# Post-norm transformer block on one core: both query halves of a step's fp32 probabilities-times-values product issued in one burst

## The reference, cut to what matters

```
result = (embeddings @ w_qkv).reshape(b, s, 3, 16, 32)
q, k, v = ...                                     # each [b, 16, s, 32]
scores = einsum('bnqd,bnkd->bnqk', q, k) / sqrt(512)
probs = softmax(scores, axis=-1)
ctx = einsum('bnqk,bnkd->bnqd', probs, v)
x = layernorm(x + ctx)
```

## Time and profile before

| what | value |
|---|---|
| median of three runs | 4508.9 us (4506.7 to 4509.33) |
| profiled execution: its span, first to last instruction | 4507.4 us (the profile gives no other time for it) |
| PE matmul busy | 4203.1 us, 93% of the span |
| DVE busy | 3206.1 us, 71% |
| ACT busy | 1857.5 us, 41% |
| L1320 (weigh), 4096 records | 531.1 + 523.5 us busy |
| L576 (maxima), 2080 records | 399.6 + 379.1 us busy |
| L492 (reductions of maxima), 2080 | 1386.7 us busy, 690 ns each |

### The profile page before, as it was taken

One profiled execution on the slowest core, in us unless ns is written; L12 is line 12 of the kernel. 1 busy time (PEld: TensorE's weight loads), 2 busy tenths in 40 slices (PEclk: granted clock), 3 DMA queues, 4 the chain that ended last, 5 costly groups with the idle time before them and its releaser, 6 DMA issues. The chain is left out here.

```text
span 4507.4 us, 59394 instructions
## 1 busy us (share of the span) xinstructions
PE 4203.1 (93%) x23081; PEld 1721.7 (38%) x23081; DVE 3206.1 (71%) x5179; ACT 1857.5 (41%) x2168; POOL 610.8 (14%) x670
## 2 busy tenths in 40 slices
PE   3499999999999999999999999999999999999999
PEld 2233344333533344333443334433353334433344
DVE  9856687667866678666876668766786667856688
ACT  3245433453334533445334543345333453344533
POOL 4300022001210012100220002200121001210022
PEclk8599999999999999999999999999999999999999
DMA  4110001010010100011001000101001010001100
GB/s 157 32 34 27 17 22 37 15 29 22 21 30 17 41 13 19 28 28 29 17 24 32 27 17 22 37 15 29 22 22 30 17 41 13 19 27 29 29 17 22
DMA packets 80509, 126.76 MB, mean 28 GB/s; under 512 B 21056, under 2 KB 23104, under 8 KB 80192
## 3 DMA queue, kind: packets, MB, share of 16 engines
q1 hardware_dynamic: 80192, 122.51, 9.4%
HBM read 53.22 MB, written 16.78 MB: 16 GB/s over the span
## 5 line engine op out<-in xcount | busy, mean ns | idle before, releaser
L492 DVE TENSOR_REDUCE mx<-R 128x1 f32<-128x512 f32 x2080 | 1386.7, 690 | 911.3 <-PE R L576 909.0
L1020 ACT ACTIVATE arena<-SC 128x1024 f32<-128x1024 f32 x1024 | 996.7, 1022 | 968.2 <-PE SC L1302 967.9
L1397 PE MATMUL SC<-wgu,split 128*128 128x512 f16 (+1 forms) x4608 | 935.5, 361 | 6.8 <-ACT split L1059 3.6
L1397 PEld LDWEIGHTS SC<-wgu,split 128*128 128x128 f16 x4608 | 445.9, 98 | 469.5 <-DVE arena L1192 10.2
L1320 PE MATMUL CT<-arena,v_even 128*33 128x512 f32 x2048 | 531.1, 606 | 9.1 <-ACT arena L1013 9.1
L1320 PE MATMUL CT<-arena 128*33 128x512 f32 x2048 | 523.5, 603 | 0.0
L1412 PE MATMUL CT<-wd,arena 128*128 128x512 bf16 x2112 | 476.7, 379 | 0.0
L946 POOL TENSOR_TENSOR x<-x,ctx_new 128x256 f32<-128x256 f32 x128 | 105.3, 823 | 2401.8 <-DVE ctx_new L1124 2401.8
L556 PE MATMUL R<-xT,wqkv 128*128 128x512 bf16 x1632 | 411.2, 385 | 1.5 <-ACT xT L454 1.3
L576 PE MATMUL R<-ks_even,qs_even 96*128 96x512 bf16 x1056 | 399.6, 400 | 8.0 <-DVE mx L492 2.9
L576 PE MATMUL R<-arena 96*128 96x512 bf16 x1024 | 379.1, 384 | 5.5
(11 more groups left out here) (111 smaller groups left out, 3749.9 us busy)
## 6 DMA issues: line engine op xcount, KB each, us to landing
x<-n_L_attn_embeddings_dram SPq DMA_DIRECT2D x136, 256.0 KB, 2.9
arena<-split SPq DMA_DIRECT2D x384, 64.0 KB, 2.0
out_dram<-x SPq DMA_DIRECT2D x64, 256.0 KB, 2.0
qs_even<-split SPq DMA_DIRECT2D x204, 64.0 KB, 2.0
ks_even<-split SPq DMA_DIRECT2D x204, 64.0 KB, 2.0
x<-in_L_ffn_w_up_dram SPq DMA_DIRECT2D x13, 256.0 KB, 2.8
x<-in_L_attn_w_qkv_dram SPq DMA_DIRECT2D x4, 768.0 KB, 6.6
x<-in_L_ffn_w_gate_dram SPq DMA_DIRECT2D x11, 256.0 KB, 4.5
```

The source lines that it names most:

```text
L492: nc.vector.reduce_max(mx[:, j:j + 1], ring_of(ring, n)[:, :], AX_X).then_inc(max_done, 1)
L1020: nc.scalar.activation(probs[:, s % 2, hd, :], SC[hd][:, :], ACT.Exp, scale=SCALE).then_inc(exp_done, 1)
L1397: last = nc.tensor.matmul(GU[kk % 2][which][:, 0:w], xhT[:, part_x * KH + k, :], wgu[:, part_w * KH + k, which * I + first:which * I + fir ...
```

## The change

`weigh` loses its argument `half` and issues both halves, four products, one after the other behind a single set of waits. It stands where the first half stood; in step 0 of a pair (from pair 1 on) that is ahead of the scores. Nothing is added or left out, and no other engine's list changes.

```diff
-                    def weigh(s, half):
+                    def weigh(s):
...
-                        if half == 0:
-                            pe.wait_ge(exp_done, 2 * s + 2)
...
+                        pe.wait_ge(exp_done, 2 * s + 2)
...
-                        key_tile, queries = step_half(p, t, half)
-                        for hd in range(2):
-                            last = nc.tensor.matmul(CT[2 * HD * hd:2 * HD * hd + HD + 1, queries * BANK:(queries + 1) * BANK],
...
-                        if half == HALVES - 1:
-                            last.then_inc(pv_done, 1)
+                        for half in range(HALVES):
+                            key_tile, queries = step_half(p, t, half)
+                            for hd in range(2):
+                                last = nc.tensor.matmul(
...
+                        last.then_inc(pv_done, 1)
...
                         if t == 0 and p >= 1:
-                            weigh(s - 1, 0)
+                            weigh(s - 1)
                             scores(p, t, 0)
                             run(places[0])
                             scores(p, t, 1)
                             run(places[1])
-                            weigh(s - 1, 1)
                             run(places[2])
                         else:
...
                             if s >= 1:
-                                weigh(s - 1, 0)
+                                weigh(s - 1)
                             run(places[2])
-                            if s >= 1:
-                                weigh(s - 1, 1)
                         run(places[3])
-                    weigh(len(steps) - 1, 0)
-                    weigh(len(steps) - 1, 1)
+                    weigh(len(steps) - 1)
```

More of the change, by code:

```diff
@@ L1306, in scores @@
                         last.then_inc(scores_done, 1)
-                    def weigh(s, half):
+                    def weigh(s):
                         p, t = divmod(s, TILES)
                         g = p // 2
-                        if half == 0:
-                            pe.wait_ge(exp_done, 2 * s + 2)
[L1314 to L1317, removed]
-                        key_tile, queries = step_half(p, t, half)
-                        for hd in range(2):
-                            last = nc.tensor.matmul(CT[2 * HD * hd:2 * HD * hd + HD + 1, queries * BANK:(queries + 1) * BANK],
-                                                    v[g % 2][:, key_tile, 2 * (p % 2) + hd, :],
-                                                    probs[:, s % 2, hd, half * BANK:(half + 1) * BANK],
-                                                    start=(key_tile == 0), stop=(key_tile == TILES - 1))
-                        if half == HALVES - 1:
-                            last.then_inc(pv_done, 1)
+                        pe.wait_ge(exp_done, 2 * s + 2)
+                        if t == 0 and g >= 1:
+                            pe.wait_ge(v_done, 2 * (ring.group(g) + 1))
+                        if t == 0 and p >= 1:
+                            pe.wait_ge(ctxT_done, p)
+                        for half in range(HALVES):
+                            key_tile, queries = step_half(p, t, half)
+                            for hd in range(2):
+                                last = nc.tensor.matmul(
+                                    CT[2 * HD * hd:2 * HD * hd + HD + 1, queries * BANK:(queries + 1) * BANK],
+                                    v[g % 2][:, key_tile, 2 * (p % 2) + hd, :],
+                                    probs[:, s % 2, hd, half * BANK:(half + 1) * BANK],
+                                    start=(key_tile == 0), stop=(key_tile == TILES - 1))
+                        last.then_inc(pv_done, 1)
                     def x_turn(i):
```

## The result

The changed kernel takes 4644.56 us (median of four runs, 4641.68 to 4646.69) against 4508.9 before: 1.0301 times as long, 95% interval 1.0286 to 1.0315. That is 136 us slower, 17 us in each of the 8 turns. The forecast was 4647 us.

A forecast was written before the change was run, and what follows sets the result against it. PE, 93% busy, was taken as the bound, with its order deciding where it waits for banks. The terms summed to 17.6 us a turn, 141 in 8 turns, less 2 hidden: 139 more, 4647 us; range 4600 to 4685.

The forecast's parts named there:

- bank time of 1.18: From a maximum's product to the next product that may use its bank: 1.18 us, DVE's 0.69 reduction included.
- pair 5: Steps 1 to 5 of this pair: +0.54 us each, 2.7 a turn; m4 starts 1.96 after m2.
- ordinary steps: 14 steps a turn: 4.65 us against 4.13, +0.52 each, 7.3 a turn.
- saved edge of 0.22: One edge of a burst fewer in a step when the two halves are joined: 0.22 us saved.
- Projection steps: 16 steps a turn: 0.30 us of waiting at the next m0 less 0.22 saved, +0.08 each, 1.3 a turn.
- Ends of pairs: Seven a turn: +0.43 us for three with a projection, +0.62 for three without, +1.32 behind pair 0; together 4.5.
- chain to neg: At a pair's end, from the start of the first of two last reductions to neg: 2.08 us, before 2.78.
- copy of CT and the exps: Behind pair ends without a projection, ACT is late for the next burst: +0.38 us, an estimate.
- wait for DMAs that the longer burst hides: Scores at a pair's start, held back by the maxima's DMAs: 2 us hidden in the whole run.
- Last pair: Its steps: +1.0 us; PE's wait for the first layer norm behind them: +0.85; sum 1.85 a turn.
- The third maximum: Rival: it doesn't wait for a bank, so 0.22 is saved in 512 steps, 112 us, 4396; chance 0.03.
- The clock: Rival: PE's clock drops to 1.2 GHz in ordinary steps and pair 5, 550 us slower, some 5060; chance 0.03.

The follow-up runs named there:

- newly dealt kernel: The kernel before with halves joined only in the 16 projection steps a turn, their maxima and projection parts dealt anew: 4486.55 us, ratio 0.9949.

## Why the prediction was right

- **The bank time of 1.18.** It was read from a place in pair 5 where two maxima and the next m0 stood together, and it is the wait between m2 and m4 in the ordinary steps and between m2 and m3 in pair 5. Shortening nothing but the reductions, from 0.69 to 0.23 us, brought it down to 0.71 and the loss of an ordinary step from 0.51 to 0.05, so for the banks that DVE empties the cause is shown, not only argued. For m4 in pair 5, whose bank ACT empties, the wait came as forecast (1.96 forecast, 1.95 measured), but no run changed ACT's copy.
- **The saved edge of 0.22** is there: 1.84 for two halves, and the newly dealt kernel keeps most of it.
- **Ordinary steps**: +0.52 forecast, +0.51 measured (4.64 for 4.13). **Projection steps**: +0.08 and +0.08 (6.80 for 6.73). **Pair 5**: +0.54 and +0.53. These are the steps in the middle of a run of their kind; at the seams a wait falls on the next step.
- **Ends of pairs**: the chain to neg 2.08 forecast, 2.07 measured. Steps 6 to 1 over pair 0 to pair 1 grew by 0.09 + 1.93 - 0.78 + 0.92 = 2.16, of which 0.51 is the ordinary step and 0.30 the projection's wait carried into step 6: 1.35 for a forecast of 1.32. The copy of CT and the exps hold up step 1 as estimated, 0.41 where 0.38 was written. All seven ends together, with the wait for DMAs that the longer burst hides, cost 4.0 a turn, where the sum has 4.5 less some 0.25.
- **Last pair**: steps 1 to 5 gained 0.94 (forecast 1.0), and from the last step to the next turn 0.75 on average (forecast 0.85).
- **The rivals.** The third maximum does wait. The clock stayed at 1.00 in a window with a wait of 0.57 us in every ordinary step and 1.03 at the neg job. The Trainium skill (TensorE: Matmul & The Clock Gate, "A second HAM failure mode: psum-queue depth-cycling") tells of a kernel whose clock swung with brief idle times of this kind; this trace shows no such swing.

The span came out 6 us under the sum (4640.0 against 4646). By the steps of the two traces, 2 us of that are step 1 of pair 0 (+0.27 instead of +0.52, from the varying step of the kernel before), 2 the end of pair 5, whose steps 6 and 7 carry xT jobs and which cost 0.17 instead of 0.43, and 1 the way into the feed-forward part; the rest is rounding. That the median met 4647 within 3 us is partly luck, since the profiled run lay 3 us below the median.

## What to carry to other kernels

Joining two halves of a product saves an edge, but a product that touches other banks is also the time in which a reader empties yours: before moving it away, measure how long a bank is taken (product to the next product that may use it) and count the jobs that now follow each other. With two banks a third job waits for the rest of that time, whatever the readers' average load says; DVE was idle 1.47 us a step, and its reductions still set the pace. Join only where other work keeps those jobs apart, and read the gain from row starts, since the entry of weight loads in a list of waits may shrink while the loss grows.

## What the runs showed of the hardware that I had not expected

A reduction of 64 columns takes 0.23 us and one of 512 takes 0.69, and two queued short ones take 0.44, so next to each other they start 0.21 apart. This shortening alone, which touches only DVE, made the kernel before 82 us faster, although PE was busy 93% of it: the waits in the prologue, at the ends of pairs, in pair 5 and in the last pair, inside a turn a fraction of a microsecond each, were worth 1.8%.
